# The recurrent stage's low-rank product with the rows stationary, and its head sums at other places in TensorE's order

## The reference, cut to what matters

```python
xa = _ln(x, ln1_w, ln1_b)
sx = concat([state[:, 1:2] - xa[:, :1], xa[:, :-1] - xa[:, 1:]], axis=1)
xxx = tanh((xa + sx * maa_x) @ maa_w1).reshape(b, l, 5, DM)   # the low-rank product, 512 -> 160
xxx = einsum('blfd,fde->blfe', xxx, maa_w2)                  # back to 5 x 512
xm = xa[:, :, None] + sx[:, :, None] * (maa_stack + xxx)
xk, xw, xv, xr, xg = (xm[:, :, j] for j in range(5))
w = exp(-exp(time_decay + tanh(xw @ td_w1) @ td_w2))
r, k, v = xr @ Wr.T, xk @ Wk.T, xv @ Wv.T;  g = silu(xg @ Wg.T)
def step(s, rkvw):                                           # 128 steps, state 16 x 16 per head
    a = k_t[..., :, None] * v_t[..., None, :]
    out = einsum('bhi,bhij->bhj', r_t, u * a + s)            # the sum over i is the "head sum"
    return a + w_t[..., :, None] * s, out
# then: head norm, * g, @ Wo.T, + x, layer norm, and a gated feed-forward of three 512 x 512 products
```

## Time and profile before

| | us |
|---|---|
| median of 3 runs | 3551.91 (3549.55 to 3552.71) |
| the profiled execution's own time | 3550.19 |
| its span in the profile | 3548.4 |
| the recurrence within the span | about 1590 to 2540 |

### The profile page before, as it was taken

One profiled execution on the slowest core, in us unless ns is written; L12 is line 12 of the kernel. 1 busy time (PEld: TensorE's weight loads), 2 busy tenths in 40 slices (PEclk: granted clock), 3 DMA queues, 4 the chain that ended last, 5 costly groups with the idle time before them and its releaser, 6 DMA issues. The chain is left out here.

```text
span 3548.4 us, 52834 instructions
## 1 busy us (share of the span) xinstructions
PE 3222.1 (91%) x19344; PEld 2128.3 (60%) x19344; DVE 1751.9 (49%) x2500; ACT 1131.8 (32%) x4052; POOL 901.4 (25%) x614
## 2 busy tenths in 40 slices
PE   7999799979999888877899999997699999799999
PEld 5665566646676555546666666675445555466675
DVE  4655456510000278864788888888264454500000
ACT  2444234421121266641332332332143343211111
POOL 2333134300000012233565555555100000100000
PEclk9999899989999999998999999999899999999999
DMA  4110231110000141111111111111130110101010
GB/s 153 52 42 26 69 136 52 43 51 21 15 21 18 45 152 50 44 33 56 34 49 36 37 48 31 42 41 33 59 126 32 33 43 20 42 18 36 21 33 12
DMA packets 103589, 168.87 MB, mean 48 GB/s; under 512 B 16433, under 2 KB 53937, under 8 KB 100017
## 3 DMA queue, kind: packets, MB, share of 16 engines
q1 hardware_dynamic: 98576, 123.27, 11.1%
q10 hardware_dynamic: 4896, 44.04, 3.1%
HBM read 133.72 MB, written 33.55 MB: 47 GB/s over the span
## 5 line engine op out<-in xcount | busy, mean ns | idle before, releaser
L2321 POOL TENSOR_TENSOR rec_S<-rec_S,rec_r_t 128x1024 f32<-128x1024 f32 x128 | 310.0, 2422 | 315.0 <-DVE rec_S L2601 315.0
L2601 DVE TENSOR_TENSOR_SCAN rec_S<-rec_decay,rec_S 128x1024 f32<-128x1024 f32 x128 | 321.9, 2515 | 22.7 <-ACT rec_S L2391 19.4
L2007 PE MATMUL mlp_bank<-mlp_src_t,region_a 128*128 128x256 f32 x1024 | 225.4, 383 | 1.7 <-ACT mlp_src_t L1932 1.7
L2007 PE MATMUL pmlp_bank<-pmlp_src_t,region_a 128*128 128x256 f32 x1024 | 224.5, 381 | 1.3 <-ACT pmlp_src_t L1932 1.3
L2019 PE MATMUL mlp_bank<-region_a,mlp_h_t 128*128 128x512 f32 x512 | 221.1, 592 | 0.0
L2019 PE MATMUL pmlp_bank<-region_a,pmlp_h_t 128*128 128x512 f32 x512 | 221.1, 592 | 0.0
L2007 PEld LDWEIGHTS mlp_bank<-mlp_src_t,region_a 128*128 128x128 f32 x1024 | 196.6, 192 | 32.4 <-issue 5.5
L2007 PEld LDWEIGHTS pmlp_bank<-pmlp_src_t,region_a 128*128 128x128 f32 x1024 | 195.9, 191 | 31.7 <-issue 5.0
L1448 ACT ACTIVATE group_scores<-group_scores,group_negmax 128x128 f32<-128x128 f32 x512 | 197.5, 391 | 29.3 <-DVE group_negmax L1542 19.3
L1977 DVE TENSOR_TENSOR mlp_y<-mlp_bank,mlp_xres 128x512 f32<-128x512 f32 x16 | 11.1, 691 | 381.0 <-PE mlp_bank L2019 381.0
L1977 DVE TENSOR_TENSOR pmlp_y<-pmlp_bank,pmlp_xres 128x512 f32<-128x512 f32 x16 | 11.1, 691 | 370.8 <-PE pmlp_bank L2019 370.8
(11 more groups left out here) (332 smaller groups left out, 6500.8 us busy)
## 6 DMA issues: line engine op xcount, KB each, us to landing
rec_vb<-v_by_head SPq DMA_DIRECT2D x32, 512.0 KB, 4.3
region_a<-in_C_w ACTq DMA_DIRECT2D x2, 4096.0 KB, 19.5
region_a<-in_G_w ACTq DMA_DIRECT2D x2, 4096.0 KB, 19.2
self_x<-in_x SPq DMA_DIRECT2D x16, 256.0 KB, 3.5
self_xres<-in_x SPq DMA_DIRECT2D x16, 256.0 KB, 2.7
rows_A<-self_xres SPq DMA_DIRECT2D x16, 256.0 KB, 2.0
cross_x<-rows_A SPq DMA_DIRECT2D x16, 256.0 KB, 3.4
cross_ctx_t<-in_ctx_t SPq DMA_DIRECT2D x16, 256.0 KB, 3.4
```

What stands on the lines that cost most here:

```text
L2007: product = nc.tensor.matmul(ph.bank(item)[:, i * TT:(i + 1) * TT], W1[:, c, f:f + 128], src_t[:, c, :, :], start=c == 0, stop=c == C - 1)
L2321: nc.gpsimd.tensor_tensor(S[u % 4][:, :, :], S[u % 4][:, :, :], bcast(r_t[:, s.k, UNITS[u][0], :], [128, JH, T], 1), ALU.mult)\
L2601: nc.vector.tensor_tensor_scan(St[:, :, :].rearrange(flat), decay[m][:, :, :].rearrange(flat), St[:, :, :].rearrange(flat), 0.0, ALU.mult, ...
```

## The change

The low-rank product is turned round. Before, the weights were stationary and 128 rows moved, in two groups of 8 `matmul` calls (128 and 32 features). After, the rows (`xa_t`) are stationary and the 160 weight columns move, in one group of 8 calls; the result has rows on the partitions. One tanh over all 160 columns writes `low_rows`, which also holds the constant ones. Three PE transposes (`low_rank_t`) bring it to PSUM bank "a" as a new item "lt" behind "mx", and three ACT copies (`low_rank_copy`) move it to `low0` to `low2`. Mixes 1 and 2 now both lie in `low0`. `mix_pair` waits on the first copy, and through `begin` for "mix2", whose bank "a" has "lt" as its last user, on all three.

Several things are moved. On PE the third quarter of the tail's `ffn_gate` stands between `low_rank_t` and `mix_pair`, its fourth quarter behind, and its first half stays at the step's end. `sum_heads` 2 goes behind the first half of `out_rows`, `sum_heads` 4 behind the second half of projection r, `sum_heads` 5 behind the second half of projection g, and `rows_t` ahead of both halves of `ffn_keys`. On DVE `normalise_front` goes ahead of `scan` 6. The host-side layout of `maa_w1` and `mix_w` follows the new order. `rows`, `out_rows`, `ffn_gate` and `ffn_values` take the chunks to do as arguments instead of a half; nothing else in them changes.

```diff
@@ -2097,12 +2097,12 @@
     head_sum = const["head_sum"]
     MIX_ORDER = [1, 2, 0, 3, 4]
     MIX_AT = {f: at for at, f in enumerate(MIX_ORDER)}
-    MIX_TILE = {0: (0, 0), 1: (0, 64), 2: (1, 0), 3: (1, 64), 4: (2, 0)}
+    MIX_TILE = {1: (0, 0), 2: (0, 64), 0: (1, 0), 3: (1, 64), 4: (2, 0)}
     JH = HS // 2
     UNITS = [(m, jh) for jh in range(2) for m in range(C)]
     NU = len(UNITS)
     NEWTON = 10
-    SETUP = 11
+    SETUP = 7
...
@@ -2121,6 +2121,7 @@
...
+        low_rows = sb("low_rows", [128, NMIX, 2 * DM])
...
@@ -2157,7 +2158,7 @@
         rec_out = ps("rec_out", [128, BANK])
         k_bank = [ps(f"k{i}", [128, BANK]) for i in range(SL)]
         banks = StepBanks("rec", sem, {b: ps(f"bank_{b}", [128, BANK]) for b in "abcdn"}, [
-            ("a", "mx", 0), ("b", "mix1", 0), ("a", "mix2", 0), ("n", "mean", 2),
+            ("a", "mx", 0), ("a", "lt", 0), ("b", "mix1", 0), ("a", "mix2", 0), ("n", "mean", 2),
             ("d", "fv", 3), ("c", "d", 0), ("n", "var", 2), ("b", "z", 0),
             ("n", "rt", 2), ("n", "nw", 2), ("a", "mix0", 0), ("b", "v", 0),
             ("c", "o", 2), ("b", "mix3", 0),
...
@@ -2420,12 +2421,16 @@
 
             def low_rank_tanh(s):
                 full(act, s, "mx")
-                for at, f in enumerate(MIX_ORDER):
-                    tile = MIX_TILE[f][0]
-                    p0, col = ((0, 64, 32, 96)[f], 0) if f < 4 else (0, T)
-                    last = nc.scalar.activation(low[tile][p0:p0 + DM, :], banks.bank("mx")[p0:p0 + DM, col:col + T],
-                                                ACT.Tanh)
-                    last.then_inc(tanh_done if at < 4 else banks.free_sem("mx"), 1)
+                nc.scalar.activation(low_rows[:, :, 0:DM],
+                                     banks.bank("mx")[:, 0:NMIX * DM].rearrange("p (f d) -> p f d", f=NMIX), ACT.Tanh)\
+                    .then_inc(banks.free_sem("mx"), 1)
+
+            def low_rank_copy(s):
+                full(act, s, "lt")
+                for tile in range(3):
+                    p = 128 if tile < 2 else 64
+                    last = nc.scalar.copy(low[tile][0:p, :], banks.bank("lt")[0:p, tile * T:(tile + 1) * T])
+                    last.then_inc(low_done if tile < 2 else banks.free_sem("lt"), 1)
 
...
@@ -2493,6 +2498,7 @@
                     first_states(middle, 1)
                 if front:
                     low_rank_tanh(front)
+                    low_rank_copy(front)
                 if middle:
                     make_decay(middle, 3)
                 if tail:
@@ -2735,10 +2741,10 @@
                     inputs(middle, 6)
                 if back:
                     mix_back(back, 0)
-                if middle:
-                    scan(middle, 6)
                 if ahead:
                     normalise_front(ahead)
...
@@ -2751,12 +2757,10 @@
 
             for tile in decay:
                 nc.vector.memset(tile[:, :, 0:1], 0.0)
-            for tile in low:
-                last = nc.vector.memset(tile[:, :], 0.0)
-            last.then_inc(zero_done, 1)
+
+            nc.vector.memset(low_rows[:, :, :], 0.0).then_inc(zero_done, 1)
             dve.wait_ge(zero_done, 1)
-            for tile, p in ((0, 32), (0, 96), (1, 0), (1, 64), (2, 32)):
-                nc.vector.memset(low[tile][p:p + 1, :], 1.0).then_inc(setup_done, 1)
+            nc.vector.memset(low_rows[:, :, DM:DM + 1], 1.0).then_inc(setup_done, 1)
...
@@ -2816,19 +2820,26 @@
                 begin(s, "mx")
                 freed(pe, s, "x")
                 pe.wait_ge(first_done, s.n + 1)
-                bank = banks.bank("mx")
                 parts = [(w, c, t) for w, t in ((maa_w1, 1), (w1_shift, 0)) for c in range(C)]
-                for lo, hi, at in ((0, 128, 0), (128, 160, T)):
-                    for n, (w, c, t) in enumerate(parts):
-                        last = nc.tensor.matmul(bank[0:hi - lo, at:at + T], w[:, c, lo:hi], xa_t[:, c, t:t + T],
-                                                start=n == 0, stop=n == len(parts) - 1)
+                for n, (w, c, t) in enumerate(parts):
+                    last = nc.tensor.matmul(banks.bank("mx")[:, 0:NMIX * DM], xa_t[:, c, t:t + T], w[:, c, :],
+                                            start=n == 0, stop=n == len(parts) - 1)
                 done("mx", last)
+
+            def low_rank_t(s):
+                begin(s, "lt")
+                for tile in range(3):
+                    p = 128 if tile < 2 else 64
+                    last = nc.tensor.transpose(banks.bank("lt")[0:p, tile * T:(tile + 1) * T],
+                                               low_rows[:, 2 * tile:2 * tile + p // 64, :].rearrange("p f d -> p (f d)"),
+                                               ident)
+                done("lt", last)
 
             def mix_pair(s, f, g):
 
                 for item in (f, g):
                     begin(s, f"mix{item}")
-                freed(pe, s, "mx")
+                pe.wait_ge(low_done, s.n * 2 + 1)
                 for c in range(C):
                     for item in (f, g):
...
@@ -2841,11 +2852,11 @@
             def mix(s, f):
                 item = f"mix{f}"
                 begin(s, item)
-                if f == 4:
-                    freed(pe, s, "mx")
+                tile, p0 = MIX_TILE[f]
+                if tile < 2:
+                    pe.wait_ge(low_done, s.n * 2 + tile + 1)
                 else:
-                    pe.wait_ge(tanh_done, s.n * 4 + MIX_AT[f] + 1)
-                tile, p0 = MIX_TILE[f]
+                    freed(pe, s, "lt")
                 for c in range(C):
                     last = nc.tensor.matmul(banks.bank(item)[:, c * 128:c * 128 + 128],
                                             mix_w[p0:p0 + 64, tile, c * 128:c * 128 + 128], low[tile][p0:p0 + 64, :],
@@ -2926,11 +2937,11 @@
...
             def step(ahead, front, middle, back, tail):
                 if front:
@@ -2962,21 +2973,25 @@
                 if back:
                     sum_heads(back, NU - 1)
                 if front:
+                    low_rank_t(front)
+                if tail:
+                    ffn_gate(tail, 2)
+                if front:
                     mix_pair(front, 1, 2)
                 if tail:
-                    ffn_gate(tail, 1)
+                    ffn_gate(tail, 3)
                 if back:
                     mean(back)
                 if middle:
                     sum_heads(middle, 0)
                 if tail:
-                    ffn_values(tail, 0)
+                    ffn_values(tail, 0, 1)
                 if front:
                     decay_low(front)
                 if back:
                     variance(back)
                 if tail:
-                    ffn_values(tail, 1)
+                    ffn_values(tail, 2, 3)
                 if middle:
                     sum_heads(middle, 1)
                 if front:
@@ -2987,14 +3002,14 @@
                     mix(front, 0)
                     project(front, "v", 2, 0)
                     project(front, "v", 2, 1)
+                if back:
+                    out_rows(back, 0, 1)
                 if middle:
                     sum_heads(middle, 2)
-                if back:
-                    out_rows(back, 0)
                 if front:
                     mix(front, 3)
                 if back:
-                    out_rows(back, 1)
+                    out_rows(back, 2, 3)
                 if front:
                     keys(front, 0)
                 if middle:
@@ -3003,30 +3018,26 @@
                     keys(front, 1)
                     mix(front, 4)
                     project(front, "r", 3, 0)
+                    project(front, "r", 3, 1)
                 if middle:
                     sum_heads(middle, 4)
-                if front:
-                    project(front, "r", 3, 1)
                 if back:
                     normed_t(back)
                 if front:
                     project(front, "g", 4, 0)
+                    project(front, "g", 4, 1)
                 if middle:
                     sum_heads(middle, 5)
-                if front:
-                    project(front, "g", 4, 1)
-                if middle:
                     bonus(middle)
-                if back:
-                    ffn_keys(back, 0)
                 if ahead:
                     rows_t(ahead)
                 if back:
+                    ffn_keys(back, 0)
                     ffn_keys(back, 1)
                 if middle:
                     sum_heads(middle, 6)
                 if back:
-                    ffn_gate(back, 0)
+                    ffn_gate(back, 0, 1)
```

More of the change, by code:

```diff
@@ L2188, in recurrence_phase @@
         shifted_done = sem("shifted_done")
-        tanh_done = sem("tanh_done")
+        low_done = sem("low_done")
         xm_done = sem("xm_done")
@@ L2737, in step @@
                     mix_back(back, 0)
+                if ahead:
+                    normalise_front(ahead)
                 if middle:
```

(30 more changed lines are left out.)

## The result

The changed kernel takes 3519.07 us (median of 4 runs, 3517.9 to 3522.02) beside 3552.31 us (3549.55 to 3555.78) of the kernel before: ratio 0.9909, 95% interval 0.9896 to 0.9921, so 33 us less. The prediction was 3523, range 3503 to 3541.

A forecast was written before the change was run, and what follows sets the result against it. A step is DVE's work plus its waits, DVE and PE waiting in turn. Thirteen steps at 1.9 us (24.7) plus 3.9 us in three earlier steps give 29 us: 3551.9 - 29 = 3523 us, range 3503 to 3541.

The forecast's parts named there:

- Part A: Turned low-rank product through mix_pair to mean: 1.4 us a step, 0.2 with a 3.5 us product, 2.0 at best.
- Part B: Head sums moved on PE: DVE's wait before mix 3 goes, 0.5 us a step, between 0 and 0.6.
- Part C: Normalisation ahead of scan 6, rows_t ahead of ffn_keys: POOL and DVE take turns, 0 to 0.1 us; upper end 1.3.
- The sum: Part A 1.4, Part B 0.5, Part C 0.05: 1.95, taken as 1.9 us a step; together 29 us.
- the slower rival: Clock falls after PE's 2.0 us gap before the product: 3.5 us more in a hit step, time 3569; chance 0.07.
- The filling steps: Three steps before 1752 with fewer stages and low clock: 1.3 us each from the shorter chain, 3.9 us.
- The thirteenth step and the draining steps: Recurrence's end: 1.9 us for the last of thirteen steps from 1752 on; nothing for draining steps, which have no front.
- the larger gain: Rival at scan 7 and shift_front: turns with POOL do not hold, 3.1 us a step, time 3502; chance 0.14.

The follow-up runs named there:

- a_only: Changed kernel with Part B and Part C taken back, so the turned low-rank product alone: ratio to the kernel before 0.9922, step 52.40 us.
- quarter_back: Changed kernel with both quarters of ffn_gate behind mix_pair: ratio to the kernel before 0.9911, step 51.97 us.
- b_only: Kernel before with only head sums 2, 4 and 5 moved: ratio to the kernel before 0.9977, step 53.18 us.
- filler: Changed kernel with one more 128x512 PE product ahead of the first half of ffn_gate: ratio to the kernel before 0.9902, step 51.65 us.
- after_no_c: Changed kernel with the normalisation and rows_t put back where they were: ratio to the kernel before 0.9896, step 51.88 us.
- c_only: Kernel before with only normalise_front ahead of scan 6 and rows_t ahead of ffn_keys: ratio to the kernel before 0.9992, step 53.61 us.
- before_bonus_late: Kernel before with only POOL's bonus product moved behind multiply 7: ratio to the kernel before 0.9997, step 53.75 us.
- bonus_late: Changed kernel with POOL's bonus product moved behind multiply 7: ratio to the kernel before 0.9871, step 50.62 us.
- late_no_c: after_no_c with POOL's bonus product moved behind multiply 7: ratio to the kernel before 0.9864, step 50.81 us.
- var_early: bonus_late with variance ahead of decay_low on PE: ratio to the kernel before 0.9860, step 50.53 us.
- all_early: var_early with rstd_t behind ffn_values' second half, mix 3 ahead of head sum 2, mix 4 ahead of keys' second half: 3490.56 us, ratio to before 0.9833.
- before_half_fr: Kernel before without the first half of the receptance product (output differs): ratio to the kernel before 1.0086, step 55.73 us.

## Why the prediction was right

**Part A was right in mechanism and nearly in size.** Forecast 1.4 us a step, measured 1.35 (a_only). The chain came out as 2.36 us of product (forecast 2.3), a tanh of 0.30, transposes of 0.55 to the last result, and three copies in 0.58 us, not 0.86: they overlapped by 0.1 us each where the five tanh had not. `mix_pair` followed the third copy's end (2112.39) by 0.17 us, as argued from the bank order. So it started at 4.27 and not 4.43, and `mean` at 6.99 and not 7.05. DVE's waits before mix 1 and `head_centre` shrank as forecast. The forecast's list of DVE's waits left out one, 1.04 us before `head_rsqrt`; it is the same before and after (12.5 us in twelve steps), so the omission cost nothing here. That the quarter of `ffn_gate` is free in the gap held, and quarter_back shows that its other place would have cost little.

**Part B was too small: 0.5 forecast, 0.6 to 0.7 measured (0.58 on the mean step of b_only, 0.7 on its undisturbed ones).** The wait before mix 3 went as forecast. The statement that the gain at head sums 4 and 5 is worth "nothing" missed that it also makes `rows_t` earlier, and with it scan 7: 0.2 us.

**Part C was right in substance: 0 to 0.1 us forecast, 0.15 and about 0 measured**, with the cause shown both ways. Scan 7 goes first, the bonus product lasts 3.26 us, `shift_front` 1.69, and moving the bonus product brings the microsecond back. The rule of the Trainium skill (GPSIMD Engine Reference, Specifications), that GpSimd contends with DVE instructions that have two SBUF inputs, now has its row for `shift_front` too: 0.67 us without and 1.69 us with the POOL product waiting ahead of it. One premise was off: the forecast set part C against the 1.36 us wait of the kernel before, while with part B in place only 0.37 us of it are left.

**The sum.** Without disturbance A and B would have given 2.1 us a step (53.75 to 51.64), not 1.9. Two of twelve steps fell to the low clock and cost 1.6 us each; this was the slower rival, and it came true in part, at less than half of the 3.5 us that I had put on it. The mean, 1.84 us, thus meets the forecast of 1.9 by two errors that offset each other; that closeness is luck, the direction is not. **The filling steps were mis-sized**: 3.9 us forecast, 7.4 measured. The product to `mix_pair` fell by 1.4, 1.4 and 2.1 us there (from 6.99, 7.13 and 8.13), where I took 1.3 each; the steps fell by 2.9, 2.3 and 2.2. a_only alone gives 7.0 us in these steps and b_only alone 2.2, so the two do not add up here, and the product is enough. What makes the first two steps fall by more than the chain stays open. In the third, more work of PE did not show: filler's extra product stands in that step too, and the step is 55.46 us long beside 55.39.

**The thirteenth step and the draining steps** gave 1.8 us together, where the forecast has 1.9 for the one and nothing for the others. Two things offset here as well. The last scan began 90.35 us after the sixteenth product instead of 94.34, so 4.0 us had been won by then, and behind that scan 2.2 us were lost again. There the last output rows took 6.44 us instead of 5.06, and from two microseconds ahead of them to the end of the recurrence the granted clock was 0.74, where it had been 0.81. So the totals, 29 us forecast and 31 measured in the spans, agree better than their terms. One rival's time does not follow the sum's own way of counting: at thirteen steps of 3.1 us and 3.9 us for the filling steps the larger gain comes to 3508 us and not 3502.

## What to carry to other kernels

In a hand-ordered pipeline, find the engine whose work and waits make up the step, and ask of each edit which of its waits it shortens. Here it was DVE, though PE was the busier one: of the 1.9 us of waits that b_only took from PE at the head sums the step kept 0.6 to 0.7, the part in which DVE had waited for PE's results, and 0.9 us of work added to PE cost nothing. Before taking a wait away, look for what stands ready to take its place: the next item in the same queue (`rstd_t` behind `variance`) or another engine's turn at the same memory (the bonus product at scan 7). And take each wait's size from the kernel in which the edit will stand, not from the one before the other edits.

## What was not expected of the hardware

An idle gap of PE of about the same length was sometimes followed by the low clock and sometimes not. With gaps of 1.8 to 2.0 us before nearly all products two of twelve steps were hit in each of after, after_no_c and quarter_back and one of twelve in b_only, at 1.5 to 1.6 us a step. With gaps of mostly 0.3 to 1.2 us (before, a_only, c_only, before_bonus_late, filler, bonus_late, late_no_c, var_early, all_early) none was; with 2.9 to 3.2 us (before_half_fr) every one, at 1.5 to 2.9 us. A longer gap did not always do it: behind 3.26 us in the draining steps of the kernel before, the four transposes of `rows_t` took 0.66 us, and behind the same gap in the kernel after 1.11. What decides was not settled.

Three ACT copies of 128x128 from PSUM took 0.58 us together, less than three times the 0.27 us of one (the copy of `c_sb` in the same timeline), while five tanh of 32x128 took 1.44 us. For the copies the Trainium skill (ScalarE: Activation LUTs, What ACT_TABLE_LOAD costs) would have given the better price: it says that ACTIVATEs back to back overlap by some 93 ns. If that holds for these rows, which the profile calls COPY, it makes 3 x 0.27 - 2 x 0.093 = 0.62 us as an estimate. The row of 0.58 us is close to it. Why the five tanh do not overlap in this way, no run here shows.
